# Low halves of the dense gelus moved from GpSimd to VectorE, gelu evaluated once, and a loop over passes written out

## The reference

```
h = W_E[x] * 16
h = h + rwkv_block(layernorm(h))                       # time mix and channel mix
h = h + moe8(layernorm(h))                             # 8 experts, width 1024, top 2 of 8
h = h + wkv_attention(layernorm(h))                    # stable WKV recurrence
h = h + block(layernorm(h))                            # 16-head causal attention, then 4 experts, top 2 of 4
  moe8:  sum_e gate_e * (gelu(y @ W1[e] + b1[e]) @ W2[e] + b2[e])
  4 experts: o0 = gelu(y@e0_up)@e0_down; o1 = silu(y@w1)*(y@w2)@e1_down;
             o2 = gelu(gelu(gelu(y@l1)@l2)@l3)@l4;  o3 = gelu(gelu(y@down)@up)@out
```

## Time and profile before

| | |
|---|---|
| median of three runs | 3157.91 us |
| profiled execution | 3164.51 us |
| its span | 3162.7 us |
| mean granted TensorE clock | 0.963 |
| PE busy | 2791.1 us (88%) |
| ACT busy | 1819.6 us (58%) |
| DVE busy | 1643.0 us (52%) |
| POOL busy | 1428.1 us (45%) |

### The profile page before, as it was taken

The page is one execution under the profiler, slowest core; times in us unless marked ns, Lnnn a source line. Parts: engine busy times, 40 slices in busy tenths (PEclk is TensorE's granted clock), DMA queues, the critical chain, the costliest instruction groups (busy, mean ns, idle before and its releaser), DMA issues. The chain is left out here.

```text
span 3162.7 us, 58694 instructions
## 1 busy us (share of the span) xinstructions
PE 2791.1 (88%) x22208; PEld 1862.8 (59%) x22208; DVE 1643.0 (52%) x3100; ACT 1819.6 (58%) x2899; POOL 1428.1 (45%) x1358
## 2 busy tenths in 40 slices
PE   3899958998999989998989898989898998987878
PEld 1555535665665666566656675667565765653555
DVE  5776735436446444644365436634563465446452
ACT  3666635555765666565565565565556655654634
POOL 5666523443454435443544454444444443453334
PEclk8999979999999999999999999999999999999999
DMA  1000028621121212121212122212222121210002
GB/s 62 21 27 13 20 74 309 239 102 66 54 92 68 78 68 93 67 82 61 96 68 82 65 81 73 89 64 74 80 82 73 66 74 61 73 41 22 24 23 76
DMA packets 59719, 235.92 MB, mean 75 GB/s; under 512 B 6560, under 2 KB 25024, under 8 KB 40640
## 3 DMA queue, kind: packets, MB, share of 16 engines
q1 hardware_dynamic: 57920, 228.13, 20.6%
q0 software_dynamic: 1536, 4.20, 0.5%
HBM read 200.57 MB, written 31.72 MB: 73 GB/s over the span
## 5 line engine op out<-in xcount | busy, mean ns | idle before, releaser
L1408 POOL TENSOR_TENSOR c_lo<-c_g,c_hi 128x512 bf16<-128x512 f32 x720 | 887.6, 1240 | 1347.0 <-ACT c_hi L1570 1222.3
L2247 PE MATMUL c_up<-c_xT,c_ring 128*128 128x512 bf16 x3072 | 750.8, 384 | 69.3 <-ACT c_hi L1570 56.0
L2264 PE MATMUL c_down<-c_ring,c_hi 128*128 128x256 bf16 x4096 | 715.4, 275 | 0.0
L1569 ACT ACTIVATE c_g<-c_up,b 128x512 f32<-128x512 f32 x512 | 352.9, 689 | 491.1 <-PE c_up L2247 487.1
L2264 PE MATMUL c_down<-c_ring,c_lo 128*128 128x256 bf16 x2048 | 563.3, 275 | 0.0
L2247 PEld LDWEIGHTS c_up<-c_xT,c_ring 128*128 128x128 bf16 x3072 | 295.7, 99 | 367.4 <-ACT c_hi L1570 67.5
L2264 PEld LDWEIGHTS c_down<-c_ring,c_hi 128*128 128x128 bf16 x4096 | 398.3, 99 | 106.0 <-issue 2.2
L1570 ACT ACTIVATE c_hi<-c_up,b 128x512 bf16<-128x512 f32 x512 | 350.9, 685 | 0.0
L1836 DVE CAST c_room<-c_room 128x384 bf16<-128x384 f32 x256 | 128.2, 530 | 403.7 <-PE c_front L2159 307.8
L1569 ACT ACTIVATE c_g<-c_up 128x512 f32<-128x512 f32 x176 | 105.5, 600 | 295.1 <-PE c_up L2000 289.0
L2264 PEld LDWEIGHTS c_down<-c_ring,c_lo 128*128 128x128 bf16 x2048 | 202.1, 99 | 25.0
(11 more groups left out here) (339 smaller groups left out, 5438.4 us busy)
## 6 DMA issues: line engine op xcount, KB each, us to landing
c_ring<-kept_dense SPq DMA_DIRECT2D x112, 1024.0 KB, 4.8
c_ring<-kept_experts SPq DMA_DIRECT2D x63, 512.0 KB, 3.4
c_room<-in_WB SPq DMA_DIRECT2D x16, 1024.0 KB, 7.0
kept_dense<-c_ring SPq DMA_DIRECT2D x16, 1024.0 KB, 4.8
c_ring<-kept_experts SPq DMA_DIRECT2D x28, 384.0 KB, 3.4
kept_experts<-c_room SPq DMA_DIRECT2D x9, 512.0 KB, 3.8
c_xT<-kept_xT SPq DMA_DIRECT2D x8, 512.0 KB, 5.2
out<-h SPq DMA_DIRECT2D x8, 512.0 KB, 6.6
```

Of the source, the lines that this page charges most:

```text
L1408: pool.tensor_tensor(lo14[:, a, :], g[:, h % 4, :], hi14[:, a, :], ALU.subtract).then_inc(lo_ready.sem, 1)
L1569: act.activation(g[:, h % 4, :], ub[n % 2][:, :], ACT.Gelu, bias=bias)
L2247: last = pe.matmul(ub[n % 2][:, :], r[:, wp, o + q * P:o + (q + 1) * P], xT[:, xp, q, :], start=(m == 0 and q == 0), stop=(m == 2 and q == ...
L2264: m = pe.matmul(bank, (hi14, lo14)[xp][:, a, s * P:(s + 1) * P], r[:, wp, o + KC * P:o + CHUNK], start=False, stop=(k == HC0 - 1 and n == ...
```

## The change

1. The low half of a U unit is made by DVE, with the same subtraction, and issued at the next U in the list (that of U(63) at D(61)). POOL keeps those of the I and G units. `lo_ready` becomes two semaphores, `lo_dense` (DVE) and `lo_expert` (POOL); `low_half` says which one to wait for.
2. ACT reads the PSUM bank once: it writes `g` with the gelu, waits for its own write (`g_ready`), and makes `hi14` by a copy of `g`. PE waits for `g_ready`, not for `hi_ready`, before it writes the bank again.
3. The loop over passes 3 to 6 is a Python loop, on all engines and for the loads: the four passes are written out with constants as semaphore targets.

```diff
@@ Plan.__init__
             if u[0] in "UI":
                 self.up[u] = len(self.bank_user)
                 self.bank_user.append(u)
+                self.gelu[u] = len(self.gelu)
@@ phase_bc, semaphores
-        hi_ready, lo_ready = (Both(x.enter_context(nc.semaphore("c_" + n)), NB, len(PLAN_C.hid))
-                              for n in ("hi_ready", "lo_ready"))
+        hi_ready = Both(x.enter_context(nc.semaphore("c_hi_ready")), NB, len(PLAN_C.hid))
+        lo_dense = Both(x.enter_context(nc.semaphore("c_lo_dense")), NB, 0)
+        lo_expert = Both(x.enter_context(nc.semaphore("c_lo_expert")), 0, len(PLAN_C.hid))
+        def low_half(i, plan, h):
+            unit = [u for u in plan.units if u in plan.hid][h]
+            if unit[0] == "U":
+                return lo_dense.sem, lo_dense.at(i, unit[1] + 1)
+            return lo_expert.sem, lo_expert.at(i, sum(u[0] != "U" for u in plan.hid if plan.hid[u] <= h))
+        g_ready = Both(x.enter_context(nc.semaphore("c_g_ready")), NB, len(PLAN_C.gelu))
@@ run (and the same for the loads on SP)
-            with eng.Fori(3, TILES - 1) as i:
+            for i in range(3, TILES - 1):
@@ GpSimd, dense
-                    if u[0] in "UIG":
+                    if u[0] in "IG":
...
-                                           ALU.subtract).then_inc(lo_ready.sem, 1)
+                                           ALU.subtract).then_inc(lo_expert.sem, 1)
@@ ScalarE, dense
                     if h >= 4:
-                        act.wait_ge(lo_ready.sem, lo_ready.at(i, h - 3))
+                        act.wait_ge(*low_half(i, plan, h - 4))
...
-                    act.activation(g[:, h % 4, :], ub[n % 2][:, :], ACT.Gelu, bias=bias)
-                    act.activation(hi14[:, a, :], ub[n % 2][:, :], ACT.Gelu, bias=bias).then_inc(hi_ready.sem, 1)
+                    act.activation(g[:, h % 4, :], ub[n % 2][:, :], ACT.Gelu, bias=bias).then_inc(g_ready.sem, 1)
+                    act.wait_ge(g_ready.sem, g_ready.at(i, plan.gelu[u] + 1))
+                    act.activation(hi14[:, a, :], g[:, h % 4, :], ACT.Copy).then_inc(hi_ready.sem, 1)
@@ VectorE, dense
+                def low(n):
+                    h, a = plan.hid["U", n], slot_of(plan, ("U", n))
+                    dve.wait_ge(hi_ready.sem, hi_ready.at(i, h + 1))
+                    dve.tensor_tensor(lo14[:, a, :], g[:, h % 4, :], hi14[:, a, :],
+                                      ALU.subtract).then_inc(lo_dense.sem, 1)
                 def step(u):
+                    if u[0] == "U" and u[1]:
+                        low(u[1] - 1)
+                    if u == ("D", NB - LAG):
+                        low(NB - 1)
@@ TensorE, bank_free
-                            pe.wait_ge(hi_ready.sem, hi_ready.at(i, plan.hid[v] + 1))
+                            pe.wait_ge(g_ready.sem, g_ready.at(i, plan.gelu[v] + 1))
@@ TensorE, down (and so in expert_up, expert_down)
                     pe.wait_ge(hi_ready.sem, hi_ready.at(i, h + 1))
-                    pe.wait_ge(lo_ready.sem, lo_ready.at(i, h + 1))
+                    pe.wait_ge(*low_half(i, plan, h))
```

More of the change, by code:

```diff
@@ L897, in __init__ @@
         self.dense, self.experts = dense, experts
-        self.up, self.bank_user, self.hid, self.group, self.gate = {}, [], {}, {}, {}
+        self.up, self.bank_user, self.hid, self.group, self.gate, self.gelu = {}, [], {}, {}, {}, {}
         n_hid = n_group = 0
@@ L1330, in _ @@
             streamed(2, PLAN_BC, PLAN_B)
-            with sp.Fori(3, TILES - 1) as i:
+            for i in range(3, TILES - 1):
                 streamed(i, PLAN_BC, PLAN_BC)
@@ L1564, in step @@
                     if h >= 4:
-                        act.wait_ge(lo_ready.sem, lo_ready.at(i, h - 3))
+                        act.wait_ge(*low_half(i, plan, h - 4))
                     elif before is not None:
-                        act.wait_ge(lo_ready.sem, lo_ready.at(i))
+                        act.wait_ge(lo_dense.sem, lo_dense.at(i))
+                        act.wait_ge(lo_expert.sem, lo_expert.at(i))
                     bias = c.b1[:, u[1]:u[1] + 1] if u[0] == "U" else 0.0
-                    act.activation(g[:, h % 4, :], ub[n % 2][:, :], ACT.Gelu, bias=bias)
-                    act.activation(hi14[:, a, :], ub[n % 2][:, :], ACT.Gelu, bias=bias).then_inc(hi_ready.sem, 1)
+                    act.activation(g[:, h % 4, :], ub[n % 2][:, :], ACT.Gelu, bias=bias).then_inc(g_ready.sem, 1)
+                    act.wait_ge(g_ready.sem, g_ready.at(i, plan.gelu[u] + 1))
+                    act.activation(hi14[:, a, :], g[:, h % 4, :], ACT.Copy).then_inc(hi_ready.sem, 1)
                 return tokens_of(i, plan, step)
@@ L1924, in gated @@
                     dve.wait_ge(up_ps.sem, up_ps.at(i, n + 2))
-                    dve.wait_ge(lo_ready.sem, lo_ready.at(i, h - 3))
+                    dve.wait_ge(*low_half(i, plan, h - 4))
                     dve.scalar_tensor_tensor(g[:, h % 4, :], sl[:, :], 0.5, ub[(n + 1) % 2][:, :], ALU.mult,
@@ L2220, in bank_free @@
                         else:
-                            pe.wait_ge(hi_ready.sem, hi_ready.at(i, plan.hid[v] + 1))
+                            pe.wait_ge(g_ready.sem, g_ready.at(i, plan.gelu[v] + 1))
                     elif before is not None and before.dense:
-                        pe.wait_ge(hi_ready.sem, hi_ready.at(i, n - 1))
+                        pe.wait_ge(g_ready.sem, g_ready.at(i, n - 1))
                     elif before is not None:
@@ L2294, in expert_up @@
                             pe.wait_ge(hi_ready.sem, hi_ready.at(i, h))
-                            pe.wait_ge(lo_ready.sem, lo_ready.at(i, h))
+                            pe.wait_ge(*low_half(i, plan, h - 1))
                     n = plan.up["I", name, k, j]
```

## The result

| | before | after |
|---|---|---|
| median | 3157.55 us | 3077.84 us |
| profiled execution | 3164.51 us | 3086.17 us |
| its span | 3162.7 us | 3084.4 us |
| mean granted TensorE clock | 0.963 | 0.969 |

After is the median of four runs, 3071.0 to 3086.17. The ratio of after to before is 0.9746, 95% interval 0.9726 to 0.9766: 80 us or 2.5% faster. In what follows a ratio to before is turned into microseconds with before's 3158.

The account below looks back on a forecast made before the run. PE's work plus its gaps bounds the kernel; the change could win gaps only. Bank -22, copy +4, low halves +8, accumulators -12 and loop -14 sum to -36 us: 3157.9 to 3122 us, range 3090 to 3154.

Parts of the forecast that it names:

- The accumulators' wait and VectorE's relief: PE's seven waits for DVE's drain (25.0 us) end some 2 us earlier each as recurrence operations shorten: -12 us (-25 to +15).
- The low halves' own waits: D units wait for DVE's low halves, chiefly at D(5) and D(13): +8 us (0 to +40).
- The loop: Passes 3 to 6 written out save three jump stops, 8.2 us, and 5.4 us within passes: -14 us (0 to -19).
- The bank: PSUM bank released at g's end, 0.57 us earlier at 46 PE waits, 85% kept: -22 us (0 to -30).
- The copy: On ACT, hi copied from g comes 0.1 to 0.3 us later, 688 times: +4 us (0 to +15).
- TensorE's clock: Granted clock left at 0.963 in the mean, since PE's work is unchanged except for less idling.
- Rival 2: VectorE becomes late from A0 to the drain, twice a pass in seven passes: +33 us, 3191 us, chance 0.12.
- Rival 1: PE waits longer for the front, giving the gain back; only the loop's 14 us stay: 3144 us, chance 0.15.

Follow-up runs that it names:

- e3_low: The kernel before with only the dense low halves moved to VectorE, one unit late: ratio to before 0.9819, -57 us.
- e6_not_low: The changed kernel with all low halves on GpSimd again (loop written out, gelu read once): ratio to before 0.9928.
- e8_pool_reads: The changed kernel plus, from pass 1, a GpSimd wait and SBUF-reading scrap subtraction per dense hidden unit: ratio to before 1.0062, 100 us slower than the changed kernel.
- e9_pool_fills: The changed kernel plus, from pass 1, a GpSimd wait and two scrap fills without SBUF reads per dense hidden unit: ratio to before 0.9796.
- e11_tiny_pool: e6_not_low with GpSimd's dense low halves cut to their first 16 of 512 columns from pass 1 on: ratio to before 0.9647.
- e10_tiny_dve: The changed kernel with VectorE's dense low halves cut to their first 16 of 512 columns from pass 1 on: ratio to before 0.9684.
- e4_not_loop: The changed kernel with its four middle passes in a hardware loop again: ratio to before 0.9823.
- e7_late_release: The changed kernel, but PE waits for the high half (the copy), not g, before writing a bank again: ratio to before 0.9791, -66 us.
- e1_loop: The kernel before with only passes 3 to 6 written out: ratio to before 0.9910, -28 us.
- e2_gelu: The kernel before with only the gelu read once (hi copied from g, bank released by g): ratio to before 0.9978, -7 us.
- v1_all_low: The changed kernel with the small experts' 208 low halves on VectorE too: median 3069.60 us, ratio to before 0.9716.

## Why the prediction was wrong

Wrong in size, right in direction: 36 us forecast, 80 measured. Step by step:

- **The accumulators' wait and VectorE's relief, -12: the step that failed.** Its own row came out as forecast, the wait fell by 10.8 us (25.0 to 14.2, 2.0 each where I had said 2). But I had used GpSimd's leaving only there and at A0. The earlier trace rows showed an operation at 0.69 and at 1.64 us depending on GpSimd alone, and I applied it to six operations of the recurrence. These give 55 of the 170 us by which VectorE's other work became shorter (131.3 to 75.9 us over the span); the other 115 are in operations that I had left out: the layernorms' scaling, the casts of the attention weights, c_ks and others. In the sum they stood at nothing, without a reason. Measured, the low halves and the relief are 57 us alone (e3_low) and 57 in company (e6_not_low), where the sum had 8 - 12 = -4. That GpSimd's reads are the cause is shown from two sides, by e8_pool_reads against e9_pool_fills and by e11_tiny_pool against e6_not_low.
- **The low halves' own waits, +8: the waits right, the cost too small.** PE waits 8.8 us for VectorE's low halves, of it 6.0 at D(12) and D(13) in passes 1 and 7 (2.5 us at each D(13), where I had 1.5), the other 2.8 in pass 0, which I had not looked at, and nothing at D(5), where I had 0.3 us in each of five passes. What they cost beyond that, by delaying other VectorE work, brings it to 20 us (e10_tiny_dve), inside the ends 0 and 40. I had feared that they would be blocked beside GpSimd's remaining low halves of the experts, for 97 us. They took 739 ns in the mean against 0.69 undisturbed; that is some 25 us over 512, an estimate.
- **The loop, -14 (0 to -19): too small.** 28 us alone and 24 in company. I had three turns at PE's own 2.8 us and half of a difference between passes. There are four places, since leaving the loop costs too, and in e4_not_loop each is 4.0 to 6.4 us, 21 in all. VectorE stands still longer there than PE does (5.5 against 2.7 us at most); that what it makes late comes on top is my reading, and the 3 to 7 us that the windows leave over stay open.
- **The bank, -22: right in mechanism, too large.** The waits came down to 67.0 us, where I had said about 70. But 12 of the 29.6 us less come with the low halves, not with the release (84.5 us in e3_low, which has no early release). The release by itself takes them from 88.8 (e7_late_release) to 67.0, 22 us, and 14 of these arrive in the time, two thirds; I had kept 85%.
- **The copy, +4 (0 to 15): too small, by what cancels the bank.** 16 us measured, for 0.09 us a unit.
- **TensorE's clock, left as it is: wrong.** It went from 0.963 to 0.969, and 22.6 of the 78.3 us of span are PE's busy time. Most of it comes with the low halves: the runs of e3_low alone have 0.970 to 0.972, and PE was busy 23.8 us less there than before (2767.3), while e1_loop has 0.965 to 0.968, e2_gelu 0.961 to 0.965 and before, beside them, 0.960 to 0.964.

The measured steps in company are 57 + 24 + 14 - 16 = 79 us; that they meet the 80 is in part luck, since the steps alone make 92; most of the disagreement is about the gelu. Rival 2, VectorE late, put a price on the right engine with the wrong sign, and its point of decision (L1695 and L1719 under 1.2 us) came out on the forecast's side at 0.74 and 0.80 in the mean. Rival 1, the gain given back, names what became of the gelu's part, but it was the copy that took it back, and whether through the front's chain is not shown.

Open: why the reads away from the recurrence still cost 0.15 us each, whether by the attention's casts, by the layernorms or by VectorE's own low halves; by what path the copy costs 16 us; and how much of a part's gain is clock, beyond the rows above.

## What to carry to other kernels

When the same operation on one engine shows two durations in a trace, find what runs beside the long ones and apply the difference to every operation of that kind, not only to the ones on the path that you happen to look at; sum it per group before and after. Work on an engine that is busy 45% of the time can be dear by what it does to another engine: here 448 subtractions cost 89 us on the emptier engine and 20 on the busier one. The same trace also says where to stop: the next 208 gave some 9 us, all of it in the last passes, and the 176 after them lost 14. And what is saved in latency by freeing a buffer early can be lost by the operation that makes it possible, so the two are measured apart.

## What the runs showed of the hardware that I had not expected

- A VectorE cast from SBUF to SBUF took 394 ns in the mean in v1_all_low, where of GpSimd's work only the attention's own low halves run beside it (median 353, up to 1074), 469 in the changed kernel, 556 beside fills and 588 beside reads; the layernorm's scaling, in the same order of kernels, 409, 780, 902 and 1008. I had thought of two-input operations alone.
- GpSimd's read of 400 columns took 1152 ns in e8_pool_reads. Between its operations of 16 columns (274 ns in e11_tiny_pool) and of 512 (1216 there), a straight line gives an estimate of 1003. By this GpSimd is held up too.
- Moving the low halves to the busier engine raised TensorE's mean granted clock: 0.971 in e3_low, which changes nothing else, against 0.963 before; 0.974 in v1_all_low.
- Leaving the hardware loop cost 4.0 us in e4_not_loop, where a turn cost 4.7 to 6.4. Between before and e1_loop the windows give 3.0 for leaving and 3.0 to 5.0 for a turn.
